# A four-stage transformer block with experts: SP's loads put in another order, waits for banks narrowed, and products of ones added on TensorE

## The reference, cut to what matters

```
x = x + tanh(g_xattn[0]) * attn0(layernorm(x), ctx, ctx)     # 16 heads of 16
x = x + tanh(g_ffn[0])   * experts(layernorm(x))             # on the first 1024 tokens' worth of rows
x = x + tanh(g_xattn[1]) * attn1(layernorm(x), ctx, ctx)     # with biases
x = x + tanh(g_ffn[1])   * quantised_ffn(layernorm(x))       # width 768

experts:  y = sum over 2 chosen of 8 experts of  weight * (gelu(x @ w1[e]) @ w2[e]),  w1: 256x1024, w2: 1024x256
quantised_ffn:  up, gate, sigmoid(gate) and both products are rounded to 16 bits with the
                largest absolute value of the whole tensor as scale; then o @ w_down.T
```

## Time and profile before

| | us |
|---|---|
| median of 3 runs | 950.01 |
| lowest, highest | 948.9, 957.11 |
| the profiled execution | 948.79 |
| its span, first to last instruction | 946.9 |
| PE busy, DVE busy, ACT busy, POOL busy in the span | 858.3, 632.0, 498.3, 160.8 |

### The profile page before, as it was taken

How to read it: one execution, slowest core, us unless ns; L and a number is a source line. 1 busy time by engine, 2 the same in 40 slices (tenths; PEclk the granted TensorE clock), 3 DMA queues, 4 the chain that set the end, 5 groups by cost and what they waited for, 6 DMA issues and landing times. The chain is left out here.

```text
span 946.9 us, 13689 instructions
## 1 busy us (share of the span) xinstructions
PE 858.3 (91%) x4092; PEld 435.7 (46%) x4093; DVE 632.0 (67%) x1264; ACT 498.3 (53%) x663; POOL 160.8 (17%) x285
## 2 busy tenths in 40 slices
PE   8789999999986999999998899999999879993098
PEld 6442333333353666666665423333333554441087
DVE  5888888888771222222357998888886568688932
ACT  1536777777741111111123577777777583597650
POOL 1233111111164000000026343000005304000000
PEclk9999999999997999999999999999999989997589
DMA  9596756564355111010138993333320000000011
GB/s 282 162 226 149 193 130 168 165 168 133 132 178 173 34 33 33 28 33 28 34 125 257 227 234 81 81 80 77 77 46 2 1 1 1 0 1 0 0 39 51
DMA packets 71325, 91.38 MB, mean 97 GB/s; under 512 B 26086, under 2 KB 56934, under 8 KB 71270
## 3 DMA queue, kind: packets, MB, share of 16 engines
q1 hardware_dynamic: 63564, 67.96, 28.4%
q0 software_dynamic: 5584, 19.93, 6.2%
q10 hardware_dynamic: 2128, 2.89, 0.9%
HBM read 62.90 MB, written 27.44 MB: 95 GB/s over the span
## 5 line engine op out<-in xcount | busy, mean ns | idle before, releaser
L1365 DVE TENSOR_REDUCE MX<-PS 128x1 f32<-128x512 f32 x512 | 320.7, 684 | 41.5 <-PE PS L1829 40.7
L976 ACT ACTIVATE Pt<-PS 128x1024 f32<-128x1024 f32 x256 | 248.2, 1021 | 102.0 <-PE PS L1850 101.9
L1829 PE MATMUL PS<-KSt,BIG 96*128 96x512 bf16 x512 | 173.7, 382 | 11.0 <-DVE MX L1365 3.9
L1850 PE MATMUL PS<-BIG,KSt 99*128 99x512 bf16 x512 | 150.0, 379 | 0.3 <-DMA BIG<-MR 0.3
L1861 PE MATMUL PS<-Pt,VS 128*17 128x512 f32 x1024 | 136.1, 598 | 0.0
L1829 PEld LDWEIGHTS PS<-KSt,BIG 96*128 96x128 bf16 x512 | 40.2, 96 | 155.2 <-DVE MX L1365 97.8
L2006 PE MATMUL PS<-BIG,KSt 128*128 x184 | 85.1, 606 | 0.6 <-DVE KSt L1489 0.4
L2028 PE MATMUL PS<-BIG,Pt 128*128 x368 | 84.2, 382 | 1.1 <-DVE Pt L1484 1.1
L1484 DVE COPY Pt<-PS 128x512 f32<-128x512 f32 x46 | 29.7, 686 | 81.4 <-PE PS L2017 81.4
L2094 PE MATMUL PS<-KSt,BIG 128*128 128x512 f32 x192 | 83.8, 597 | 0.0
L1033 ACT ACTIVATE Pt<-PS 128x512 f32<-128x512 f32 x46 | 27.5, 597 | 89.1 <-PE PS L2006 89.1
(11 more groups left out here) (203 smaller groups left out, 1038.6 us busy)
## 6 DMA issues: line engine op xcount, KB each, us to landing
qk_parts<-BIG SPq DMA_DIRECT2D x64, 192.0 KB, 3.2
BIG<-in_w POOLq DMA_DIRECT2D x12, 1024.0 KB, 5.5
BIG<-qk_parts SPq DMA_DIRECT2D x32, 192.0 KB, 3.3
KSt<-qk_parts SPq DMA_DIRECT2D x32, 192.0 KB, 3.8
v_rows<-BIG SPq DMA_DIRECT2D x8, 544.0 KB, 4.8
VS<-v_rows SPq DMA_DIRECT2D x32, 136.0 KB, 3.0
BIG<-qk_parts SPq DMA_DIRECT2D x32, 128.0 KB, 3.9
KSt<-qk_parts SPq DMA_DIRECT2D x32, 128.0 KB, 4.0
```

What stands on the lines that cost most here:

```text
L976: act.activation(PP[:, 2 * (kc % 2) + half, :, :].rearrange("p h t -> p (h t)"), ST[half], ACT.Exp, scale=DK ** -0.5).then_inc(exp_done, 1)
L1365: dve.tensor_reduce(MX[:, g % 2, i % TB, i // TB:i // TB + 1], ring(i), AX.X, ALU.max, negate=True).then_inc(max_taken, 1)
L1829: pe.matmul(ring(i), QS[0:ROWS, g, h, qc * P:(qc + 1) * P], KS[0:ROWS, g, h, :], start=True, stop=True).then_inc(max_done, 1)
L1850: last = pe.matmul(ST[half][:, i * S:(i + 1) * S], KS[0:ROWS + PARTS, g, h, kc * P:(kc + 1) * P], QS[0:ROWS + PARTS, g, h, :], start=True, ...
```

## The change

It does six things. SP loads w2 of expert 4 as soon as the first 8 tiles have been turned, then issues the two slot loads when the scatters have landed, and only then waits for the other tiles and projections to load w2 of expert 5 and WO. DVE's normalisation of group 2 in layer 0's last batch goes behind update 6 and the third pair. `project_out` waits for all earlier updates only within attention (tiles 1 to 7); tile 11 waits for update 7, and the tiles behind it for the update four tiles before. PE issues 14 products of ones behind the last tail's copy and before the first slot tile is turned. It issues 20 products of ones when the ninth of the second twelve products on DVE is done, before the fifth spread of a maximum. And it issues 8 more behind that spread.

```diff
@@ sync
             sp.wait_ge(st_done, 8 * NG * B)
             for e in (6, 7):
                 load_w2(sp, e, w2_late)
-            sp.wait_ge(tro_done, NT)
-            for e in (4, 5):
-                load_w2(sp, e, w2_late)
-            sp.wait_ge(out_done, NT)
-            sp.dma_start(WO[:, :, :], io["attn_w"][1, 3].rearrange("(c p) n -> p c n", p=P)).then_inc(wo_in, 16)
+            sp.wait_ge(tro_done, EARLY)
+            load_w2(sp, 4, w2_late)
...
             sp.wait_ge(scattered, 16 * TOPK * ROUTED)
             load_slots(0, 0, 0)
             load_slots(0, 1, 1)
+            sp.wait_ge(tro_done, NT)
+            load_w2(sp, 5, w2_late)
+            sp.wait_ge(out_done, NT)
+            sp.dma_start(WO[:, :, :], io["attn_w"][1, 3].rearrange("(c p) n -> p c n", p=P)).then_inc(wo_in, 16)
             load_biases(sp, 1)
@@ vector, last_group_3
                 pair_begin(2)
-                normalise(NG * n + 2, B - 1, 2, LAST_OUT)
                 update(0, 6, 5)
                 pair_end(2)
+                normalise(NG * n + 2, B - 1, 2, LAST_OUT)
@@ tensor, project_out
-                if to == 5 and i > 0:
+                if 0 < i < EARLY:
                     pe.wait_ge(x_upd, t)
                 elif i == EARLY + 3:
                     pe.wait_ge(x_upd, NT * layer + EARLY)
@@ tensor, before the experts
+            pe.wait_ge(on_evac, NT)
+            keep_busy(14, bank(0)[:, 0:P])
             turn_slots(0, 0, 0)
             turn_slots(0, 1, 0)
-            pe.wait_ge(on_evac, NT)
             pe.wait_ge(x_upd, NT)
@@ tensor, before the down projection
             spread_max(3, 0, 7)
+            pe.wait_ge(prod_done, 2 * PIECES - 2)
+            keep_busy(20, bank(5)[:, 0:P])
             spread_max(4, 0, 7)
+            keep_busy(8, bank(5)[:, 0:P])
             pe.wait_ge(qwt_ready, 9)
```

## The result

The changed kernel takes 940.77 us (median of four runs, 939.02 to 942.21) against 951.80 us before (four runs, 948.9 to 957.11): a ratio of 0.9888, 95% interval 0.9859 to 0.9917. It is faster by about 11 us, just inside the upper end of the range that was given (932 to 941), and some 5 us above the predicted 935.5. The profiled execution took 942.21 us with a span of 940.3.

The account below looks back on a forecast made before the run. TensorE is busy nearly everywhere, so time is in three seams: before the experts, layer 1's tail, before the down projection. 10.1 + 2.0 + 2.3 = 14.4 us off 948.79 gives 934.4; with the median 1.2 above, 935.5 us, range 932 to 941.

Parts of the forecast that it names:

- the first seam: From first attention to experts: first hidden product 7.9 us sooner, plus 2.2 us from full clock, together 10.1 us.
- the last scatter's landing: End of layer 0's attention: last scatter issued at 282.7, landing after 2.5 us, at 285.2.
- the way from the slots to the first hidden product: Start of experts: slots land, turning 0.4 us, copy 0.45, then issue; first hidden product at 288.4 against 296.31.
- layer 1: Projection tail after layer 1's attention: projection 11 starts sooner without its wait; gain 2.0 us, bounds 1.0 and 2.1.
- the down projection: Its start: twenty and eight products of ones keep the clock up; gain 2.8 us if it holds, 2.3 taken.
- The moved normalise: DVE, layer 0's last batch: delays last turning, fourth pair, its scatters and updates 8 to 11 by 1.0 us (0.3 to 1.5).
- The last projection and the products of ones: Before the experts: projections end at about 284.2, fourteen products take 3.0 us, to 287.3, just until the slots land.
- rival 1: Before the experts: w2 of expert 5 is the new wait, or the ones run cold; 939 us, chance 0.17.
- the first expert tile waits for w2, after the first hidden product: Start of experts: w2 of expert 5 lands at 291.8, first hidden product ends at 292.0, so no cost, by 0.2 us.
- rival 2: Before the down projection: the clock falls again and the gain there is 0; 938 us, chance 0.16.
- Rival 3: Before the experts: last scatter lands 7 us later, queued behind w2 of expert 4; 942.6 us, chance 0.06.
- Rival 4: Expert stage: without the earlier rest the chip grants half clock for a while; 965 us with 60 us of it, chance 0.03.

Follow-up runs that it names:

- the two pairs: Profiles of the kernel before and the changed kernel, both run again for the second: changed 940.77 us, then 938.27 us, ratio 0.9888 each time.
- the last pair: Kernel before with SP's order, early third slot load, layer 1's wait and 28 products, against the whole change again: 950.11 and 950.27 us, beside 962.80 before.

## Where the prediction failed: the first seam of its sum

The direction and the three places of the gain were right, and the median lies just inside the range. The mechanism of the first seam was not sized right, and by the prediction's own sign ("the forecast fails if the experts' start moves by less than 7 us") it failed: counted from the first projection, the first hidden product moved by 6.3 us in the first pair of profiles and by 6.7 in the second, where 7.9 were forecast. The steps that failed are the last scatter's landing (3.3 us, not 2.5), the way from the slots to the first hidden product (1.6 us, not 1.1), and the gain from the first to the third hidden product, taken as a sure 2.2 us of clock with nothing late behind it (1.0 and 0.4 us in the two pairs). Two more of its signs of being wrong are there, a slot load that lands 6.7 us after its issue, and half clock in the first down tile. The sum was 14.4 us; by the traces it is 7.3 in the first seam (10.1 expected), 2.6 in layer 1 (2.0) and 2.2 to 2.9 at the down projection (2.3), together 12 to 13, and the medians moved by 11.0, 12.2 and 12.5 in three comparisons. (Of the 5.3 us between 935.5 and 940.77, 1.8 are the start of the sum: the kernel before took 951.80 beside the changed one, where the sum had started from 950. What the traces of single executions leave over is not traced.) What was too large is the first seam, in these terms:

- *The moved normalise.* 1.0 expected, 1.2 found. Mechanism as described (turning at 277.05 waits for it).
- *Scatter to slot loads.* The step "lands after 2.5 us" failed: 3.3, by 0.7 over the 2.6 that the sum had. A packet of instruction code falls into this stretch and the scatter's last packets start only at its end; without the fourteen products it doesn't fall there, and the scatter lands after 2.4.
- *The last projection and the products of ones.* The projections ended 1.2 us after the last scatter's issue, close to what was expected (284.2 against 282.7). The fourteen take 3.29 us, 3.0 expected. My reading of the earlier trace rows was wrong in itself: 28 rows are fourteen products, 0.43 us each, and in the first seam, at full clock, each takes 0.235 us. That the page's clock row says full at the start proves nothing: the trace's first entry of the clock there is a rise to full at 7.09 us. Two errors made one nearly right number.
- *Slots to the first hidden product.* The step "turning 0.4 + copy 0.45 + issue" counted one tile's half; two are turned and copied (DVE's copies take 0.96 us together), and the second lands 0.5 us after the first. 1.6 us instead of 1.1.
- *The second hidden product.* The 5.2 us at full clock hold where the clock does (5.3 to 5.4). But the clock fell in five of the nine profiles in which products of ones end just ahead of the slots' landing; then it is 6.9 to 7.5. The sum took the full 2.2 us of the clock and priced no chance of that; rival 1 had the ones "run cold", but through their own length.
- *What is late next.* The step "the first expert tile waits for w2, after the first hidden product" had the order wrong. The first product with w2 is at 303.50, behind *two* hidden products and the third slot tile, 12.6 us after w2's issue; its landing is not in this trace, and was 5.5 to 6.1 us after the issue in the nine others of this order that have it, close to the 5.5 that was forecast. Rival 1's price was about right for the wrong transfer: what comes late is the third slot load, the last of a row that begins with w2, WO, the biases and the next layer's weights. It costs 0.9 to 1.3 us in the three profiles of this order behind the fourteen in which the clock holds, and nothing where the clock falls. The Trainium skill, "DMA: Bandwidth & Descriptors", section "Two DMAs through the same engine are not ordered", gives no promise that a later transfer ends later; in this trace the late one took 6.7 us behind those ahead of it, against 2.1 and 2.2 for the first two.

The first hidden product 1.6 us later than forecast and 1.2 us less from the clock and the third load: that is the 2.8 of 10.1 that is missing. *Layer 1* gave 2.6 and not 2.0, as I had counted the wait of 1.85 us and not the last projection's 0.67. *The down projection* gave what was said, in another way: rival 2's fall happened in the changed kernel (892.9), and yet it took but 0.8 us (first tile 3.37 us, a later one 2.59), since the clock was back within 3.4 us (896.3), during the first tile. In the profile without the 28 products the first tile takes 5.5 us and the second is late as well. Rival 3 came true for 0.7 us of its 7, and with another cause: beside w2 of expert 4 the ninth to thirteenth scatter took 6.2, 6.0, 5.6, 4.9 and 3.0 us (before 5.1, 4.1, 3.5, 2.6 and 2.4), but the fourteenth and fifteenth 2.4 again. Rival 4 fell: from the third hidden product to the last go 160.9 to 161.9 us in every profile, whatever came before. The low end of the range was added up wrong: its terms (0.5 at the end, 1.0 for the normalise, 0.1 in layer 1 on top of 14.4) make 16.0, so 934 and not 932.

The largest surprise is in what the parts are worth. In layer 0 the move, the wait and the fourteen together cost 2.2 to 2.7 us of the seam against SP's order alone (2.0 in the last pair, which has the early third load on one side); with that order alone the seam is 9.4 us shorter than before, and the rest pays in layer 1 and before the down projection. Why the clock falls behind the fourteen in some executions and not in others is open: the rest ahead of the turning doesn't sort them (full after 1.15, 1.20, 1.29 and 1.43 us, fallen after 0.78, 1.01, 1.18, 1.22 and 1.29). That the packet of code delays the scatter rests on the packets' times; it was not tried by moving code alone, and whose code it is was not looked up.

## What to carry to other kernels

When a load is let go earlier, look at the whole row of transfers behind it: the next small one that the consumer needs, not the large one beside it, was the new wait here. Late work of the same engine that ends just when the data lands kept the clock in both profiles that had it, products of ones that ended ahead of the landing in four of nine; hurrying it and putting products of ones behind it gained nothing here, while the same edit gained its full 2.6 us in layer 1, where the engine is what sets the end. Compare parts by the length of their own stretch in the trace, as the whole time scattered by more than the parts are worth.

## What the hardware showed that was not expected

- One packet of instruction code (queue 8, 16 KB) in the stretch of a scatter's landing goes with 0.9 us more to its landing (3.3 against 2.4 us): three of the scatter's 96 packets start only at its end. The Trainium skill, "Runtime: NRT & Kernel Launch", section "Instruction fetch mechanics", has the sequencer fetch code in 16 KiB blocks over a DMA queue of its own at a cost that is mostly hidden. The packet's size agrees; the cost here was not hidden, as it fell to another transfer, the scatter.
- The granted clock fell behind 3.3 us of dense products and 1.01 us of rest, and stood behind the same products and 1.43 us; at 1.29 us it did each once.
- The products of ones at the kernel's start took 0.43 us each, in the first seam at full clock 0.235. The page shows full clock for that slice, but the trace has no entry of the clock before a rise to full at 7.09 us. In the 16 profiles that first entry comes at 4.7 to 7.2 us, and the later it comes, the longer the fourteen take (4.9 to 6.1 us).
- The last scatter landed 5 us later (7.4 instead of 2.4) with 2 MB of w2 and 0.25 MB of WO issued from 0.5 us ahead of it to 1.2 us behind.
